# A graph kernel's sums: edge weights multiplied into the gathered rows, plain selections made once by VectorE, constant row slots

## What is computed

```python
def gcn_conv(x, src, dst, ew, W, b):
    deg = jax.ops.segment_sum(ew, dst, num_segments=N)
    dis = jnp.where(deg > 0, jax.lax.rsqrt(jnp.maximum(deg, 1e-12)), 0.0)
    norm = dis[src] * ew * dis[dst]
    h = x @ W
    out = jax.ops.segment_sum(norm[:, None] * h[src], dst, num_segments=N)
    return out + b
...
h = jax.nn.relu(gcn_conv(x, src, dst, ew, W1, b1))      # 64 columns: the first sum
z = jax.nn.relu(gcn_conv(h, src, dst, ew, W2, b2))      # 32 columns: the nodes phase
...
e = jax.nn.leaky_relu(a1[src] + a2[dst], negative_slope=ALPHA)   # attention, softmax over
out = jax.ops.segment_sum(msg, dst, num_segments=n)              # the edges of each dst
```

## Time and profile before

| what | value |
|---|---|
| median of 3 runs | 9729.46 us (9718.26 to 9732.11) |
| the profiled execution | 9720.19 us, span 9718.4 us |
| busy: PE, PEld, DVE, ACT, POOL | 5162, 3761, 3941, 2471, 5208 us |
| granted clock of TensorE, mean | 0.626 of 2.4 GHz |
| DMA queue of the gathers (q0) | 200912 packets, 351 MB, 15.2% of the engines' span |

### The profile page before, as it was taken

One profiled execution on the slowest core, in us unless ns is written; L12 is line 12 of the kernel. 1 busy time (PEld: TensorE's weight loads), 2 busy tenths in 40 slices (PEclk: granted clock), 3 DMA queues, 4 the chain that ended last, 5 costly groups with the idle time before them and its releaser, 6 DMA issues. The chain is left out here.

```text
span 9718.4 us, 105437 instructions
## 1 busy us (share of the span) xinstructions
PE 5161.7 (53%) x20322; PEld 3761.4 (39%) x20322; DVE 3940.9 (41%) x11819; ACT 2470.5 (25%) x5095; POOL 5208.3 (54%) x5326
## 2 busy tenths in 40 slices
PE   3533333333333356665665656465566666556469
PEld 3533333332333244444444444343334343334336
DVE  6433333332333122222222222366666667667601
ACT  2522332222233011111111111233333333333211
POOL 1266655555554555555555554366566666666241
PEclk6555555555555566666666666666666667666679
DMA  4233333333333222222222222255555555555220
GB/s 133 77 106 104 109 105 105 104 100 98 98 105 110 64 60 64 65 63 63 65 71 62 64 63 63 85 161 160 155 166 171 163 169 169 160 162 169 89 71 19
DMA packets 638167, 1018.09 MB, mean 105 GB/s; under 512 B 175792, under 2 KB 308376, under 8 KB 636918
## 3 DMA queue, kind: packets, MB, share of 16 engines
q0 software_dynamic: 200912, 351.35, 15.2%
q1 hardware_dynamic: 282662, 450.37, 14.3%
q10 hardware_dynamic: 154000, 209.63, 6.2%
HBM read 709.70 MB, written 327.09 MB: 107 GB/s over the span
## 5 line engine op out<-in xcount | busy, mean ns | idle before, releaser
L1736 POOL DMA_INDIRECT att_rows<-ft_rows,edges x1760 | 1837.2, 1044 | 1210.3 <-PE att_pm L1949 516.5
L806 POOL DMA_INDIRECT nod_rows<-table,sources x1688 | 1600.2, 948 | 1304.4 <-issue 1060.2
L806 POOL DMA_INDIRECT conv_rows<-table,sources x1688 | 1599.9, 948 | 1204.5 <-issue 933.2
L1019 PE MATMUL conv_pm<-conv_rows,conv_sel 128*128 x3520 | 942.3, 430 | 1752.5 <-issue 1448.0
L1949 PE MATMUL att_pm<-att_rows,att_sel 128*128 128x264 f32 x3520 | 1465.2, 565 | 493.2 <-issue 360.1
L1019 PEld LDWEIGHTS conv_pm<-conv_rows,conv_sel 128*128 128x128 f32 x3520 | 809.0, 323 | 1889.4 <-issue 1887.5
L1949 PEld LDWEIGHTS att_pm<-att_rows,att_sel 128*128 128x128 f32 x3520 | 879.2, 273 | 860.4 <-issue 493.0
L969 DVE TENSOR_TENSOR acc<-acc,conv_pm 128x64 f32 x1760 | 388.3, 221 | 1684.4 <-remote 985.8
L1190 PE MATMUL nod_pm<-nod_rows,nod_sel 128*128 x3520 | 649.4, 333 | 684.9 <-issue 364.5
L1443 DVE TENSOR_TENSOR acc<-acc,nod_pm 128x32 f32 x1760 | 330.8, 188 | 1676.1 <-issue 720.6
L1190 PEld LDWEIGHTS nod_pm<-nod_rows,nod_sel 128*128 128x128 f32 x3520 | 627.2, 258 | 775.2 <-issue 764.1
(11 more groups left out here) (406 smaller groups left out, 6455.4 us busy)
## 6 DMA issues: line engine op xcount, KB each, us to landing
selections<-conv_hot ACTq DMA_DIRECT2D x220, 512.0 KB
weighted_selections<-conv_sel SPq DMA_DIRECT2D x440, 256.0 KB
nod_sel<-weighted_selections SPq DMA_DIRECT2D x440, 256.0 KB
att_sel<-selections SPq DMA_DIRECT2D x440, 256.0 KB
att_bc<-places SPq DMA_DIRECT2D x110, 512.0 KB
att_rows<-ft_rows,edges POOLq DMA_INDIRECT x1760
conv_rows<-table,sources POOLq DMA_INDIRECT x1688
nod_rows<-table,sources POOLq DMA_INDIRECT x1688
```

Of the source, the lines that this page charges most:

```text
L806: pool.indirect_dma_start(out=rows[:, k % SLOTS, :], out_offset=None, in_=table, in_offset=bass.IndirectOffsetOnAxis(ap=K.srct[:, k:k + 1] ...
L1019: ins = nc.tensor.matmul(pm[i % RING][:, k, :], sel[:, i % RING * QUAD + k, :], rows[:, ds(slots[k], 1), :].rearrange("p a c -> p (a c)"), ...
L1736: pool.indirect_dma_start(out=rows[:, k % SLOTS, :], out_offset=None, in_=K.ftd, in_offset=bass.IndirectOffsetOnAxis(ap=sources[:, k:k + 1 ...
```

## The change

- In both sums each step has a gather of its own: 1760 instead of 1688. Step s lies in slot s mod 128, which is a constant in the program. `K.spack`, `quad_slots`, `arrived_by` and the part of `schedule` that counted gathers are gone; `sources` is a third copy from the same transposed block (ScalarE makes three copies of each of the 14 blocks instead of two, and the later pass with its 14 gathers and transposes is gone).
- VectorE's selections are plain (compare only), and SP stores them to `K.seld`, from where both `nodes` and `attention` load. ScalarE makes none in `first_sum`. `K.selw` is gone.
- New `weigh(q)`: one VectorE multiply of a quad's gathered rows by the edge weights, in place, 128x256 in the first sum, 128x128 in nodes. It waits for `arrived`, and TensorE now waits for it. It stands a quad ahead: in the first sum between the selections of q + 1 and the adds of q, in nodes ahead of the adds of q.
- `segment_flags` is no phase any more: its three loads are issued by SP at the start of `first_sum`, VectorE does its work after 9 of the first group's 18 quads, and SP stores the results with one small store in each of 18 quads from quad 36 on.

```diff
@@ schedule @@
-            for c in range(4):
-                own.did(dve.tensor_copy(tilef[0:1, c * CH:(c + 1) * CH], rowp[0:1, c, 0:CH]))
...
-            own.then(ts(K.spack[0:1, :], steps4[:, :, 0], SLOTS - 1, None, ALU.bitwise_and))
...
+                act.activation(K.srct[:, i * P:(i + 1) * P], src_t[:, 0, :], ACT.Copy)
                 act.activation(K.ew[:, i * P:(i + 1) * P], src_t[:, 2, :], ACT.Copy).then_inc(tp_free, 1)
@@ gather_rows @@
-    counted = [arrived_by(q * QUAD + QUAD - 1) for q in range(QUADS)]
-    for j in range(0, GATHERS, SECT):
-        free = j + SECT - SLOTS + LEAST * GROUPS
-        if free > 0:
-            pool.wait_ge(mm_done, free)
+    for j in range(0, STEPS, SECT):
+        if j >= SLOTS:
+            pool.wait_ge(mm_done, j + SECT - SLOTS)
         if j >= LANES:
-            pool.wait_ge(arrived, 1 + next(q for q in range(QUADS) if counted[q] >= j + SECT - LANES))
+            pool.wait_ge(arrived, (j + SECT - LANES) // QUAD)
@@ first_sum, SyncE @@
+                if FLAGS_FROM <= q < FLAGS_FROM + len(flag_stores):
...
+                    sp.dma_start(to, of).then_inc(flags_out, 16)
                 sp.wait_ge(sel_ready, q + 1)
-                sp.dma_start(K.selw[q], sel[:, q % RING * QUAD:(q % RING + 1) * QUAD, :].rearrange("p i n -> p (i n)")
+                sp.dma_start(K.seld[q], sel[:, q % RING * QUAD:(q % RING + 1) * QUAD, :].rearrange("p i n -> p (i n)")
@@ first_sum, VectorE @@
-                    ins = dve.tensor_scalar(sel[:, slot * QUAD + i, :], K.iota[:, :], K.edges[:, 1, ds(s, 1)],
-                                            K.ew[:, ds(s, 1)], ALU.is_equal, ALU.mult)
+                    ins = dve.tensor_scalar(sel[:, slot * QUAD + i, :], K.iota[:, :], K.edges[:, 1, ds(s, 1)], None,
+                                            ALU.is_equal)
                 ins.then_inc(sel_ready, 1)
+
+            def weigh(q):
+
+                s = q * QUAD
+                dve.wait_ge(arrived, q + 1)
+                r = rows[:, s % SLOTS:s % SLOTS + QUAD, :]
+                tt(r, r, K.ew[:, s:s + QUAD].unsqueeze(2).to_broadcast([P, QUAD, C]), ALU.mult).then_inc(weighted, 1)
...
                     select((i + 1) % RING, t * (TURN_QUADS // RING) + (i + 1) // RING, s + QUAD)
+                    if q + 1 < QUADS:
+                        weigh(q + 1)
                     dve.wait_ge(mm_done, s + QUAD)
@@ first_sum, TensorE (nodes alike, with row_weighted) @@
-                    slots = quad_slots(pe, K, q)
                     pe.wait_ge(sel_ready, q + 1)
-                    pe.wait_ge(arrived, q + 1)
+                    pe.wait_ge(weighted, q + 1)
                     for k in range(QUAD):
                         ins = nc.tensor.matmul(pm[i % RING][:, k, :], sel[:, i % RING * QUAD + k, :],
-                                               rows[:, ds(slots[k], 1), :].rearrange("p a c -> p (a c)"),
-                                               start=True, stop=True)
+                                               rows[:, (q * QUAD + k) % SLOTS, :], start=True, stop=True)
```

More of the change, by code:

```diff
@@ L291, in _ @@
             own.did(ts(stepx[0:G, :], stepf[0:G, :], begin, None, ALU.is_ge))
-            own.did(stt(out=gat[:, :], in0=ranks[:, 0:1], scalar=float(-LEAST), in1=begin, op0=ALU.mult, op1=ALU.add))
             own.wait()
@@ L297, in _ @@
                 op1=ALU.mult).then_inc(inside_ready, 1)
-            own.did(stt(out=gat_until[:, :], in0=gat[:, :], scalar=float(-LEAST), in1=steps, op0=ALU.add, op1=ALU.add))
-            own.did(tt(tile_jump[:, :], tiles_before, gat[:, :], ALU.subtract))
-            own.did(tt(back_jump[:, :], gat[:, :], tiles_before, ALU.subtract))
-            own.did(ts(named[:, :], K.iota[0:G, 0:G], ranks[:, 0:1], None, ALU.is_equal))
+            own.then(ts(named[:, :], K.iota[0:G, 0:G], ranks[:, 0:1], None, ALU.is_equal))
+            dve.sem_inc(named_ready, 1)
             dve.wait_ge(jumped, 1)
@@ L316, in _ @@
             own.did(ts(nwin[:, :], K.wcol[:, :], float(-P), None, ALU.mult))
-            dve.wait_ge(tau_done, 1)
-            own.then(tt(tauf[:, :], pos[:, :], tp[1][:, 8:8 + SB], ALU.add))
-            ts(taui[:, :], tauf[:, :], float(TB * P - 1), None, ALU.min).then_inc(tau_ready, 1)
+            dve.wait_ge(order_done, 1)
             own.did(dve.tensor_copy(K.order[:, :], tp[1][0:1, 32:32 + G]))
@@ L335, in _ @@
                 own.then(tt(K.wpack[0:1, :], K.wpack[0:1, :], shifted[0:1, :], ALU.bitwise_or))
-            dve.wait_ge(places_done, 1)
-            for c in range(4):
-                own.did(tt(trow[0:1, c * CH:(c + 1) * CH], tilef[0:1, c * CH:(c + 1) * CH], rowp[0:1, c, 0:CH],
-                           ALU.add))
-            own.wait()
-            steps4 = trow[0:1, :].rearrange("a (q i) -> a q i", i=QUAD)
-            own.then(ts(K.spack[0:1, :], steps4[:, :, 0], SLOTS - 1, None, ALU.bitwise_and))
-            for i in range(1, QUAD):
-                own.then(ts(shifted[0:1, :], steps4[:, :, i], SLOTS - 1, WBITS * i, ALU.bitwise_and,
-                            ALU.logical_shift_left))
-                own.then(tt(K.spack[0:1, :], K.spack[0:1, :], shifted[0:1, :], ALU.bitwise_or))
             dve.wait_ge(gathered, 16 * SB)
@@ L811, in rows_arrived @@
 def rows_arrived(sp, q, gathered, arrived):
-    for k in range(arrived_by(q * QUAD - 1) if q else 0, arrived_by(q * QUAD + QUAD - 1)):
+    for k in range(q * QUAD, (q + 1) * QUAD):
         sp.wait_ge(gathered[k % LANES], 16 * (k // LANES + 1))
@@ L876, in first_sum @@
         sel_stored = [ph.sem(f"sel_stored{q}") for q in range(RING)]
-        taken, sel_ready, mm_done, added, arrived, apart, made = (
-            ph.sem(x) for x in ("taken", "sel_ready", "mm_done", "added", "arrived", "apart", "made"))
+        taken, sel_ready, weighted, mm_done, added, arrived = (
+            ph.sem(x) for x in ("taken", "sel_ready", "weighted", "mm_done", "added", "arrived"))
+        keys_in, flagged, flags_out = ph.sem("keys_in"), ph.sem("flagged"), ph.sem("flags_out")
         loaded, biased, turned, kept, table_done, scaled, table_stored, chain, passed = (
@@ L915, in segment @@
                 act.activation(ht[:, :], pt[:, :], ACT.Relu).then_inc(kept, 1)
-                at, count = section_at(j), section_at(j + 1) - section_at(j) if more else 0
-                sections(t, at, min(LATER, count))
                 act.wait_ge(scaled, n + 2)
@@ L920, in segment @@
                               ).then_inc(table_stored, 16)
-                sections(t, at + LATER, max(0, count - LATER))
             turns(act, segment)
-            for h in range(HALF):
-                act.wait_ge(stored[h], 16 + STEPS // SECT // HALF * 16)
             act.wait_ge(table_stored, 16 + GROUPS * 16)
@@ L948, in _, with flags @@
             tt = dve.tensor_tensor
+            def flags():
+                own.did(dve.memset(flb[:, :, :], 0.0))
+                dve.wait_ge(keys_in, 48)
+                own.then(tt(fl[:, :, :], ks[:, :, 1:P + 2], ks[:, :, 0:P + 1], ALU.not_equal))
+                own.then(dve.tensor_scalar(fl[:, :, :], fl[:, :, :], NEG, None, ALU.mult))
+                own.did(dve.tensor_copy(flb[:, :, 0:P + 1], fl[:, :, :]))
+                for i in range(2):
+                    own.did(dve.tensor_reduce(th[:, i, :], fl[:, :, i:i + P], AX.X, ALU.min))
+                own.wait()
+                dve.sem_inc(flagged, 1)
             def select(slot, lap, first):
@@ L1190, in products @@
                         ins = mm(pm[bank][:, k, :], sel[:, slot * QUAD + k, :],
-                                 rows[:, ds(slots[k], 1), :].rearrange("p a c -> p (a c)"), start=True, stop=True)
+                                 rows[:, ((q + i) * QUAD + k) % SLOTS, :], start=True, stop=True)
                     ins.then_inc(mm_done, QUAD)
@@ L1514, in _ @@
             dve.sem_inc(added, QUAD)
+            weigh(0)
             add(0, 0, FIRST[0])
```

177 lines of the change are left out of this document (48 added, 129 removed).

## The result

The changed kernel takes 9784.8 us (median of 7, 9760.7 to 9854.8), the kernel before beside it 9736.9 (7 runs, 9718.3 to 9758.5): a ratio of 1.0062, 95% interval 1.0041 to 1.0084. It is slower, by 48 us between the medians and 60 us by the ratio, where 9705 us and rather a gain were forecast. The profiled execution after took 9760.7 us (span 9759.0), 41 us more than the one before.

The account below looks back on a forecast made before the run. Waits bound the kernel: the first sum cycles between quick gathering and slow register instructions on TensorE and VectorE. Terms -15 - 37 + 5 + 104 - 180 + 64 + 15 + 20 = -24 gave 9705 us at the median; range 9200 to 9990.

Parts of the forecast that it names:

- Setup: Before the first sum: shorter schedule -15 us, and the flags' own phase gone, -37 us.
- the drag: Both sums: stretches, after some 9.5 us of unbroken gathering, in which register instructions of TensorE and VectorE turn slow.
- First sum: First sum: 72 more gathers, TensorE's register instructions gone, multiply on VectorE; net +104 us, bounds +40 and +190.
- the prediction's own balance: First sum: steps gathered per cycle equal steps done by quads; 1.54 us a step before, 1.598 with the change.
- S: First sum: us of gathering under the drag in each cycle, 26.9 before and 27.9 forecast with the change.
- TensorE's relief: Both sums: TensorE's 15 register instructions a quad go; first sum's slow quad 13.46 to 12 us, nodes -180 us.
- Nodes, -180 + 64 + 15: Nodes phase: TensorE's register instructions gone -180 us, multiply on VectorE +64, 72 more gathers +15.
- The multiply beside GpSimd, +20: Both sums: gathers slowed by the new multiplies with two SBUF inputs, +20 us (0 to 96).
- Rival A: Both sums: joint count of TensorE and VectorE register instructions starts the drag, now after 19 us; 9301 us; chance 0.20.
- B: Both sums: the drag vanishes, first sum at GpSimd's 1.25 us pitch (-542 us), nodes -300; 8860 us; chance 0.07.
- D: Both sums: whole-stream stall, TensorE's matmuls stay slow, removed phases pay for the 72 gathers; about 9730 us; chance 0.03.
- C: Both sums: VectorE's slow quad of 16 us becomes the bound, none of nodes' 180 returns; 9973 us; chance 0.25.

## Why the prediction was wrong

- *Setup*: -57 to the first gather, and -50 without the drag, against -52 with the flags' own work of +5 taken apart. Right.
- *First sum*: +104 and 5 for the flags, measured +91. The total is near, and two of its terms are not: the undragged quad came at 3.04 us and not 3.27 (1492.69 to 1495.73 above), and the dragged quad at 13.3 us and not 12. With both put right the prediction's own balance gives S = 29.1 and +84. So the agreement is luck: two errors cancelled.
- *TensorE's relief*: the step that failed. The prediction divided the dragged quad of 13.46 us, less the matmuls, by TensorE's 15 register instructions, and took some 1.5 us off each dragged quad of the first sum and 180 us of nodes for taking them away. The runs showed that the quad doesn't hang on them: with all 15 gone it is 13.27 us, and VectorE's stand for `mm_done` in the first sum went from 965 to 931 us. The 14 of VectorE that were to take 0.75 us each mostly don't: 469 of its 5728 sequencer records in the first sum took over 0.6 us. In nodes TensorE's issue wait fell by 156 us, but 411 us of wait for the multiply came in, and VectorE's stand for `mm_done` there rose from 530 to 653 us.
- *Nodes, -180 + 64 + 15*: these terms carry the sign, and the runs don't part them. I put 72 more gathers at 15 us because GpSimd stands 40% of the stretch; in the first sum the same gathers were in the balance with their full weight. After the change the pitch is 2876.5/1759 = 1.635 us against 2842.2/1687 = 1.685. Priced at the pitch, the gathers are 72 x 1.635 = +118, and all the rest is 1688 x -0.05 = -84 (predicted -180 + 64 = -116); with 118 in place of 15 the whole sum is +79 on the profiled execution, against 41 measured there and some 60 by the ratio. That is a way to book the 34 us and not a measurement: with 15 for the gathers and 64 for the multiply as forecast, a relief of 45 in place of 180 gives the same 34. Without the drag the same 72 gathers cost 92 us in nodes by direct removal, where GpSimd sets the pace; with it their cost was never measured alone.
- *The multiply beside GpSimd, +20*: a gather grew by 7 ns in the first sum and 1 in nodes, 12 and 2 us of an engine that stands over 1100; without the drag the gathers took 3 ns less beside the multiplies in the first sum and 4 more in nodes (949 and 954 against 952 and 950). My price, 0.31 us lost per us, came from attention's longer gathers, 1037 to 1048 ns over all runs; that they are longer because of L2059 was not shown, and its rows are longer too. By the Trainium skill, "GPSIMD Engine Reference", section "1. Specifications", the multiply's two SBUF inputs should contend with GpSimd; for multiplies of 0.28 and 0.42 us in each 5 us the runs show at most 7 ns a gather.
- *Rival A*, one budget for both engines, falls, as far as the two cycles looked at show: with half of the register instructions the drag still came 10 to 11 us after GpSimd resumed, not 19. *B* falls: the drag stayed. *D* came nearest by its number (about 9730, a cost of nothing), but its mechanism falls, as TensorE's matmuls are in one piece. *C* had the side right and the place half right: the TensorE waits for the multiply are there (1151 and 411 us), VectorE's dragged quad has the 13.3 us at which C begins to decide, but not 16; and in nodes "none of 180 comes back" is near what the second booking above says (45).

What stays open: what the drag is. It is not the chip alone: one and the same chip had the kernel before at 7750 us and, some minutes later, at 9710. It is not the kernels: it lies on both, and both ran without it. One thing sets the runs apart that was not followed up, the recording itself: the four traces with the drag hold 31520 to 33117 semaphore raises by transfers, the sixteen without it 115280 to 121148, though the number of transfers is about the same. The drag may cost the trace these records, writing them may be what holds the engines up, or a third thing may do both; no run tells which. The times of `mm_done` above rest on the records that were kept, 296 in the first sum after the change. Whether a wider pitch of the gathers keeps the drag off, and what the parts of the change are worth under it one by one, wasn't measured either.

## What to carry to other kernels

A wait that the trace puts down to "remote" was ended by a semaphore: look up which one, who raises it, and when that engine's work ended. Where raise and work lie apart, 10 us here, the neighbour's own instructions are not what costs the time, and taking them away gave next to nothing back. Where two engines work lists side by side, taking work from the shorter one was worth 1%, and computed addresses on the longer one are dear (1.7 us a quad here). Where an engine never stands, each more of its instructions costs its full pitch (89 and 92 us for 72 gathers); for one that stands 40% of a stretch these runs don't give the price, so a forecast whose sign hangs on it should carry both prices.

## What the runs showed of the hardware that I had not expected

- The same program took 7750 or 9710 to 9740 us; nothing in between was seen. In the slower runs 1161 of 6428 records of TensorE's sequencer and 407 of 5728 of VectorE's took over 0.6 us (trace of the kernel before, first sum; the median is 0.05 us), and the semaphore that matmuls raise is recorded a median of 8.5 us (before) and 6.5 us (after) after they ended, where VectorE stands for it.
- The traces of the slower runs hold about a quarter of the semaphore raises by transfers that those of the others hold (31520 to 33117 against 115280 to 121148).
- A semaphore update costs 0.093 us on VectorE's sequencer and 0.151 on TensorE's, in rows of 60; on GpSimd four of them fit into the 0.30 us between two gathers.
- TensorE's sequencer starts on the updates behind a quad 0.03 us after the quad's first matmul when the matmuls have constant addresses, and 1.70 us after it when each address is computed (9.31 against 11.02 us a quad).
- In the changed kernel, matmuls of constant addresses were untouched by the drag: 1.94 us for eight.
